# The last cross attention and the last self attention in one block: the second one's weights, first input and front products placed inside the last batches of the first

## The reference

```
x = _layernorm(x + _L1_attn_ref(x, ...))
x = _layernorm(x + _L1_xattn_ref(x, ctx_1024, Wq, Wkv, Wout, bout))   # stage L1x below
x = _layernorm(x + _L1_ffn_ref(x, ...))                                # stages L1s and moe below
# inside _L1_ffn_ref
h = rmsnorm(X, norm1_w)
q, k, v = h @ wq, h @ wk, h @ wv                   # 16 heads of 16
attn = softmax(q k^T * scale); ctx = attn @ v
X = X + ctx @ wo                                   # all of this is stage L1s
h2 = rmsnorm(X, norm2_w); logits = h2 @ router_w   # the expert part: stage moe
```

## Time and profile before

| | |
|---|---|
| time, median of 3 runs | 2084.19 us (2082.79 to 2084.83) |
| the profiled execution | 2084.06 us |
| its span | 2082.2 us |
| PE busy | 1768.5 us (85% of the span) |
| DVE, ACT, POOL busy | 55%, 49%, 35% |
| mean granted clock of PE | 0.923 |

### The profile page before, as it was taken

The page is one execution under the profiler, slowest core; times in us unless marked ns, Lnnn a source line. Parts: engine busy times, 40 slices in busy tenths (PEclk is TensorE's granted clock), DMA queues, the critical chain, the costliest instruction groups (busy, mean ns, idle before and its releaser), DMA issues. The chain is left out here.

```text
span 2082.2 us, 40894 instructions
## 1 busy us (share of the span) xinstructions
PE 1768.5 (85%) x15132; PEld 1418.1 (68%) x15132; DVE 1143.6 (55%) x3113; ACT 1010.0 (49%) x2377; POOL 732.7 (35%) x642
## 2 busy tenths in 40 slices
PE   6888875888849999949999999588859996999994
PEld 5777664666539898837777777466547775788883
DVE  3656664356446454444555555445558772457774
ACT  4555551354325454444555555255436662356663
POOL 2334342677322423232333333221124442334433
PEclk9999996799669999979999999899869997999997
DMA  2000002000062524350000000111010415723334
GB/s 68 12 12 13 20 6 79 1 14 25 18 226 81 162 82 121 98 163 1 11 11 12 11 11 6 42 30 32 17 54 17 135 37 188 250 85 52 52 52 101
DMA packets 97899, 125.47 MB, mean 60 GB/s; under 512 B 8586, under 2 KB 84826, under 8 KB 97674
## 3 DMA queue, kind: packets, MB, share of 16 engines
q1 hardware_dynamic: 84410, 105.09, 15.3%
q0 software_dynamic: 13296, 17.77, 5.0%
HBM read 85.03 MB, written 39.89 MB: 60 GB/s over the span
## 5 line engine op out<-in xcount | busy, mean ns | idle before, releaser
L1932 POOL TENSOR_TENSOR L1a_probs<-L1a_probs,L1a_rinv 128x1024 f32<-128x1024 f32 x64 | 121.3, 1896 | 270.1 <-DVE L1a_rinv L2247 270.1
L1929 POOL TENSOR_TENSOR L0a_probs<-L0a_probs,L0a_rinv 128x256 f32<-128x256 f32 (+1 forms) x128 | 103.2, 828 | 191.0 <-DVE L0a_rinv L2247 191.0
L2239 DVE CUSTOM_DVE_ANT_0 L1a_sbias<-L1a_psS,L1a_bias 128x256 f32<-128x256 f32 x256 | 93.2, 421 | 109.0 <-PE L1a_psS L2040 109.0
L2192 ACT ACTIVATE L1a_probs<-L1a_sbias,L1a_nmx 128x256 f32<-128x256 f32 x256 | 126.6, 498 | 47.5 <-DVE L1a_nmx L2239 47.4
L2919 POOL DMA_INDIRECT moe_sums<-moe_y,moe_xg x39 | 80.1, 2053 | 138.3 <-DVE moe_y L3218 111.1
L2192 ACT ACTIVATE L0a_probs<-L0a_sbias,L0a_nmx 128x128 f32<-128x128 f32 (+1 forms) x256 | 112.8, 443 | 28.8 <-DVE L0a_nmx L2239 28.8
L2503 POOL DMA_INDIRECT ec_sums<-ec_yk,ec_token_at x32 | 59.0, 1845 | 189.5 <-ACT ec_yk L2624 184.6
L2689 DVE TENSOR_TENSOR ec_h<-ec_sg,ec_psU 128x512 f32<-128x512 f32 x64 | 43.9, 687 | 119.1 <-ACT ec_sg L2611 119.1
L2997 PE MATMUL moe_psY<-moe_wts,moe_hT 128*128 (+1 forms) x440 | 104.0, 379 | 0.8 <-ACT moe_hT L3064 0.8
L2536 PE MATMUL ec_psG<-ec_xs,ec_wt 128*128 128x512 f32 x384 | 99.0, 394 | 2.1 <-issue 2.1
L2239 DVE CUSTOM_DVE_ANT_0 L0a_sbias<-L0a_psS,L0a_later 128x128 f32<-128x128 f32 (+1 forms) x256 | 76.2, 354 | 44.4 <-PE L0a_psS L2037 44.0
(11 more groups left out here) (540 smaller groups left out, 5001.6 us busy)
## 6 DMA issues: line engine op xcount, KB each, us to landing
shelf<-in_L_ffn_w_gate SPq DMA_DIRECT2D x8, 1024.0 KB, 9.3
shelf<-in_L_ffn_w_up SPq DMA_DIRECT2D x8, 1024.0 KB, 13.1
ec_wd<-in_L_ffn_w_down SPq DMA_DIRECT2D x8, 1024.0 KB, 6.3
moe_rows<-blank SPq DMA_DIRECT2D x1, 5070.0 KB, 19.5
moe_xg<-moe_rows SPq DMA_DIRECT2D x39, 130.0 KB, 2.1
moe_wts<-in_L_ffn_e_gate SPq DMA_DIRECT2D x8, 512.0 KB, 9.6
moe_wts<-in_L_ffn_e_up SPq DMA_DIRECT2D x8, 512.0 KB, 9.4
moe_wts<-in_L_ffn_e_down SPq DMA_DIRECT2D x8, 512.0 KB, 9.5
```

The source lines that it names most:

```text
L1929: last = pool.tensor_tensor(v, v, bcast(rinv[:, r, :, t], 2, KEYS[t]), ALU.mult)
L1932: last = pool.tensor_tensor(v, v, bcast(rinv[:, r, :, :].rearrange("p h t -> p (h t)"), 2, S), ALU.mult)
L2192: ins = act.activation(probs[:, r, j, at], sbias[:, g % 2, j, at], ACT.Exp, bias=nmx[:, r, j, t:t + 1], scale=-1.0, accum_out=sums[:, r, j ...
L2239: last = dve.tensor_tensor_reduce(out=sbias[:, g % 2, j, at], in0=psS[:, slot + j, at], in1=added, scale=-1.0, scalar=LARGE, op0=ALU.add, ...
```

## The change

L1s no longer has a block of its own. `self_programs` holds the five streams of the old `self_stage` as generators, and `context_stage` gets them as `follow`: each of its streams advances the matching generator by one piece (`next(tail, None)`) at fixed steps, and runs the rest of it at its end. The call for the cross attention only notes its arguments; the call for the self attention builds both.

- SP: norm1 and wq are loaded after L1x's batch 0 is stored, the other weights after batch 1, x of L1s's batches 0 to 3 after batches 2 to 5.
- POOL scales the weight rows and makes the low parts (before: DVE), after steps 15 to 25; `root_front(0)` after step 29.
- ACT makes the high parts after steps 18, 19, 21 and 22, and `scale_x(0)` after step 30; xT, qk 0, `keep_queries` and the rest stand between the last pieces of L1x, the last `finish` behind `exponential(0, 0)` of L1s.
- DVE takes `front_stats(0)` after step 28, xT after step 31, the two qk and the first maxima between the last pieces of L1x.
- PE turns x inside step 31 and makes qk 0, qk 1, v and the first scores between the last pieces of L1x; the two last `out` items stand behind the first scores.
- Bare storage is shared: L1s's masks, keys, values, y, xn and so on lie in buffers of L1x, and both stages use one set of the eight accumulation banks. L1x (and L0x, which is built by the same function) gets its two item banks and its bank for turned maxima from other bank numbers. L1s's vs memset and first `mark_keys` wait for L1x's last values.
- In L1x `finish(B - 2)` comes ahead of the last `out_high`, and DVE's `set_off(B - 2)` ahead of the last `out_low`.

```diff
-def context_stage(nc, name, kind, consts, x_in, x_out, w, gate_w=None, aff=None):
+def context_stage(nc, name, kind, consts, x_in, x_out, w, gate_w=None, aff=None, follow=None):
...
+        POOL_HOOKS = (9, 15, 17, 21, 22, 23, 25, 29)
+        ACT_HOOKS = (18, 19, 21, 22, 30)
+        DVE_HOOKS = (28, 31)
...
             values(N - 1)
+            next(tail, None)
             turn_values(N // 2 - 1)
+            next(tail, None)
             turn_back(N // 2 - 1)
+            next(tail, None)
             item(("out", 0), B - 1)
             item(("out", 1), B - 1)
...
+            for _ in tail:
+                pass
...
             copy_values(N // 2 - 1)
+            next(tail, None)
+            if not rope:
+                finish(B - 2)
+            next(tail, None)
             out_high(N // 2 - 1)
-            for b in (B - 2, B - 1):
+            next(tail, None)
+            for b in (B - 2, B - 1) if rope else (B - 1,):
                 finish(b)
...
+    def sync_program(sp):
...
+        sp.dma_start(raw[:, :, 0:D], w["wq_t"].rearrange("(c p) k -> p c k", p=P)).then_inc(wq_in, 16)
+        yield
+        sp.dma_start(raw[:, :, D:3 * D], w["wkv_t"].rearrange("(c p) k -> p c k", p=P)).then_inc(wkv_in, 16)
...
+        yield
+        for b in range(RX - 1):
+            load_x(b)
+            yield
...
+    def gpsimd_program(pool):
...
+        pool.wait_ge(norm_in, 16)
+        scale_rows(slice(0, D), wq_in, HD ** -0.5)
+        yield
+        scale_rows(slice(D, 3 * D), wkv_in, 1.0)
+        yield
+        for j in range(2):
+            at = slice(j * D, (j + 1) * D)
+            low_part(wqk[:, 1, :, at], raw[:, :, at], wqk[:, 0, :, at], j + 1)
+            yield
+        low_part(wv[:, 1, :, :], raw[:, :, 2 * D:3 * D], wv[:, 0, :, :], 3)
+        yield
+        low_part(wo[:, 1, :, :], raw_o[:], wo[:, 0, :, :], 4)
+        yield
+        pool.wait_ge(halves, 1)
+        root_front(0)
+        yield
+        pool.wait_ge(prev["k_ready"], 2 * prev["steps"])
+        pool.memset(vs[:, :, :, :, 1:3, :].rearrange("p r t h e d -> p (r t h) (e d)"), 1.0).then_inc(ones_set, 1)
+        pool.wait_ge(prev["v_done"], prev["steps"])
+        prev["wait_taken"](pool, ("v", B // 2 - 1), 0)
+        mark_keys(0, 0)
+        mark_keys(0, 1)
+        root_front(1)
+        yield
...
+        wait_taken(pe, ("v",), 0)
+        scores(0, 0)
+        yield
+        wait_taken(pe, ("qk", 1), 0)
+        for t in range(2):
+            prev["wait_taken"](pe, ("out", t), B - 1)
+        scores(0, 1)
+        turn_top(0)
+        scores(1, 0)
...
+        row_max(0, 0)
+        front_stats(1)
+        row_max(0, 1)
+        yield
+        shift(0)
+        row_max(1, 0)
+        yield
...
     elif kind == "cross":
-        context_stage(nc, name, kind, consts, x_in, x_out, w)
+        consts[6].append((name, kind, x_in, x_out, w))
     else:
-        self_stage(nc, name, consts, x_in, x_out, w, extra_out)
+        held_name, held_kind, held_in, held_out, held_w = consts[6].pop()
+        context_stage(nc, held_name, held_kind, consts, held_in, held_out, held_w,
+                      follow=partial(self_programs, nc, name, consts, x_in, x_out, w, extra_out))
```

More of the change, by code:

```diff
@@ L689, in _ @@
                 item(what, b)
+            for _ in tail:
+                pass
         @block.scalar
         def _(act):
+            tail = rest.scalar(act) if rest else iter(())
             def take(what, b):
```

1078 lines of the change are left out of this document (546 added, 532 removed).

## The result

| | before | after |
|---|---|---|
| median, 4 runs each, one chip | 2084.51 us (2082.79 to 2085.81) | 2064.51 us (2060.86 to 2067.38) |
| span of the profiled execution | 2082.2 us | 2064.9 us |
| granted clock, mean | 0.923 | 0.927 |

The ratio is 0.9919, with a 95% interval of 0.989 to 0.9947. The changed kernel is faster, by 17 us (11 to 23) by the ratio; the two medians lie 20.0 us apart.

What follows compares the result with a forecast made beforehand. PE, busy 85% of the span, bounds the kernel except at the L1x to L1s seam, where it stands still. First exponential 15.5 us earlier, less 0.5, gives 2084.06 - 15.0 = 2069.1 us; range 2063.5 to 2076.5.

Steps and rivals of the forecast that it cites:

- A: Seam from L1x to L1s: gain as forecast, 13 to 18 us, time 2066 to 2071 us; chance 0.63.
- C: PE around the seam: the clock does not fall at all, gain 20 to 23 us, 2061 to 2064; chance 0.09.
- Weight work on POOL at no cost: L1x's loop: weight scalings and low parts move from DVE to POOL, done batches before PE needs them, cost nothing.
- rival E: POOL beside DVE: 10.6 us of hold-off, 2079.7 us, or gain given back at moe's start; no real change; chance 0.06.
- Pieces in the loop, +1.4: L1x's loop: ACT's piece after step 21 +0.3 us, DVE's statistics after step 28 +1.1; bounds 0 and 2.2.
- Clock back by qk 1: PE in the seam: maybe 2.4 GHz by qk 1, three products 1.67 us each, 3.4 us saved.
- the two ends: L1s's first exponential: 1536.3 at low clock (13.9 us earlier) or 1532.9 with clock back (17.3); middle 15.5 taken.
- Clock stays: PE in the seam: clock at 0.50 from 1496 to somewhere in 1514 to 1520; 0.50 past 1520 would show error.
- The chain through ACT's queue: Seam: ACT's queue ends with v at 1523.8, then PE's scores and outs, DVE's y and maxima; first exponential 1536.3.
- `finish` behind the exponential, 0.5: ACT behind L1s's first exponential: L1x's last finish, 1.09 us, shares a gap with xT's copy; 0.5 us subtracted.
- Rival B: Seam: one chain through ACT's queue and low clock into L1s lose 5 us; gain 6 to 12, 2072 to 2078; chance 0.18.
- Rival D: L1x's loop: added pieces make PE's clock fall earlier, up to 2.1 us a step, slower overall; chance 0.04.

Runs made afterwards that it cites:

- Experiment 4: Changed kernel with DVE's first statistics split behind steps 26 and 27 and ACT's high part of wv behind step 20; ratio 0.991 to the kernel before.
- third profile: Changed kernel run a third time, no edit; ratio 0.991 to the kernel before.
- Experiments 8: Changed kernel with ACT's finish late, L1s's maxima earlier, statistics split, and unread filler matmuls in steps 28, 29 and the seam; 2075.87 us, ratio 0.9866.
- 10: The kernel of Experiments 8 (reordered, with filler) run again, no edit; 2048.98 us, ratio 0.9839 to the kernel before.
- 9: Changed kernel in its own order, with filler matmuls in steps 28 and 29 and 8 more in the seam; 2059.36 us, ratio 0.9906 to the kernel before.
- second profile of the changed kernel: Changed kernel run again, no edit; 2081.49 us, ratio 0.9884 to the kernel before of its set.

## Why the prediction was right

2069.1 was predicted, within 2063.5 to 2076.5, and 2064.5 measured. The gain of 17 us by the ratio lies in A's 13 to 18; the median itself lies between A's 2066 to 2071 and C's 2061 to 2064, though C's mechanism, a clock that doesn't fall, did not come. The place of the gain, the seam, and its form were right. That the number came so near is in part luck: the loop cost more than in the sum and the products less, and a low clock that the sum did not expect any more was in its prices all the same. One slip of the sum itself: the unknown costs span 2065.5 to 2072.1, not 2071.5. Term by term:

- **Weight work on POOL at no cost: right.** The exponentials of steps 18 to 21 stand 0.70 to 0.72 us ahead of before's throughout (1446.17 against 1446.87 at the start of step 18, 1461.34 against 1462.06 at the end of 21), with POOL's scalings at 1426 to 1444 and its first two low parts at 1460 to 1462. DVE and POOL side by side did not hold each other off by anything that these marks show, so rival E's 10.6 us did not come. The work itself was also less than that: by its rows 0.94 and 1.36 us for the four scalings and 2.51, 1.26 and 1.28 for the four low parts, 7.35 in all. The last two low parts lie behind step 21, and from the second exponential of step 22 to the first of step 28 the distances are before's within 0.03 us.
- **Pieces in the loop, +1.4: too small.** They cost 0.28 at step 22, as said (0.3), and 1.92 by step 30 in place of 1.1. That is the bound of 2.2 that I had set aside. I had given the wait of PE for the maximum 0.5 us of slack; the whole 1.7 us of statistics came through, and the fall of the clock, some 0.4 us sooner against the work, went with it. Experiment 4 shows that the wait wasn't necessary; its clock fell where before's did. The 4.1 us a step that I gave for steps 18 to 28 is that of steps 22 to 26; over all ten it was 4.26 us before, and is 4.29.
- **Clock back by qk 1: earlier, in this execution.** It came back ahead of qk 0, with `out`, values, the turn back and xT as the work before it, at 1509.5. The three products took 1.7 us each, all of the 3.4 us between the two ends, of which I had taken half. This is the term that was mis-sized: 1.7 us. The pieces between the products, which both ends of the sum had at 1.2 GHz, gave another 1.3: from the start of the turn back to the end of v I had 13.4 us (1508.06 to 1521.5), and it took 8.7 (1508.15 to 1516.84). When the clock comes back is not a constant of the kernel: in the third profile qk 0 and most of qk 1 ran at 1.2 GHz, and the seam took 1.2 us more.
- **Clock stays: wrong.** I expected 0.50 up to 1514 or 1520 and then no more, and had named 0.50 past 1520 as a sign of being wrong. It fell again at 1520, in PE's wait of 2.52 us or just behind it, and stayed to 1537. Scores, outs and the first steps of L1s ran at 1.2 GHz, as my sum had them by accident: I had costed the outs at 2.90 (they took 2.93) for the low clock that I then let end. Experiments 8 and 10 show that it need not fall when the order leaves shorter waits and PE has filler; in 9, filler without the order, it fell.
- **The chain through ACT's queue: right in its order,** with 1.86 us of waiting for `off` ahead of `finish`, v taken as the last thing that PE's first scores wait for, and the maximum behind both y. From the end of v on PE to the exponential I had 14.8 us (1521.5 to 1536.3), and it took 15.1 (1516.84 to 1531.92). Predicted was 1532.9 to 1536.3 on the axis of before; it is 1532.6, the changed kernel's 1531.92 and the 0.70 by which its step 18 comes sooner, so just ahead of the range.
- **`finish` behind the exponential, 0.5:** the third and fourth exponentials of L1s are 6.70 and 8.96 us behind the first, before 6.40 and 8.65. So it is 0.3.
- **Rival B** had the two facts right, one chain through ACT's queue and a low clock that lasts into L1s, and their price wrong, for the low clock was there before as well. **Rival C** needed the filler and the reordering; the change alone did not keep the clock. **Rival D** is not settled: in the second profile of the changed kernel the clock fell 17.5 us behind the first exponential of step 24, and 24.1 in the only profile of the kernel before, and the stretch to step 30 took 0.7 us more than in the first. Whether L1s's pieces in the loop had a part in that was not tested; it came nowhere near the 15 us that D needs.

In the profiled pair, 17.5 us of the gain lie between the marks, 0.4 came from an earlier step 24, and 1.0 was lost behind L1s, where the code is the same (357.4 and 358.4 us from L1s's last exponential to the end). The remaining 0.4 is in the rest of L1s.

## What to carry to other kernels

Where one stage ends and the next begins, count PE's pauses and not only the work: the last batch of a pipelined loop has no next batch to prepare, PE thins out there, and the clock falls before the seam is reached. The next stage's first products belong in those steps, and if there are too few of them, matmuls that nobody reads (here 24 of some 0.15 us) can pay, once no queue puts other work ahead of what PE waits for. Between the marks they gave 4 to 6 us in the changed kernel, which its whole time does not show, and 9 in the reordered one, whose whole time does. In an engine's queue at a seam, what the old stage still has to finish goes behind what the new stage's first step needs.
